# Feed-forward weights quantised in the first attention, sums added a step later, and smaller buffer rings

## What is computed

```python
x = x + L0_xattn(layernorm(x), ctx_1024, mask, ...)   # 16 heads of 64, 6272 keys, masked
x = x + L0_attn(layernorm(x), ...)
x = x + L0_ffn(layernorm(x), ...)                     # 8 experts, 2 chosen
x = x + L1_xattn(layernorm(x), ctx_1024, ...)         # 6272 keys, then 64 keys
x = x + L1_attn(layernorm(x), ...)                    # gated delta rule
x = x + L1_ffn(layernorm(x), W_in, b_in, W_out, b_out)

def quantize_w8_per(w, axis):                         # used by L1_ffn alone
    amax = jnp.clip(jnp.max(jnp.abs(w), axis=axis, keepdims=True), 1e-08, None)
    scale = 127.0 / amax
    return jnp.clip(jnp.round(w * scale), -128.0, 127.0) / scale
```

## Time and profile before

| | us |
|---|---|
| median of 3 executions | 407.27 |
| lowest and highest | 406.82 and 411.14 |
| profiled execution, its own time | 406.98 |
| span of the profile | 405.1 |
| PE matmul busy | 383.4 |
| ACT busy | 287.2 |
| DVE busy | 276.8 |
| POOL busy | 256.4 |

### The profile page before, as it was taken

One profiled execution on the slowest core, in us unless ns is written; L12 is line 12 of the kernel. 1 busy time (PEld: TensorE's weight loads), 2 busy tenths in 40 slices (PEclk: granted clock), 3 DMA queues, 4 the chain that ended last, 5 costly groups with the idle time before them and its releaser, 6 DMA issues.

```text
span 405.1 us, 11383 instructions
## 1 busy us (share of the span) xinstructions
PE 383.4 (95%) x4529; PEld 280.0 (69%) x4529; DVE 276.8 (68%) x715; ACT 287.2 (71%) x568; POOL 256.4 (63%) x207
## 2 busy tenths in 40 slices
PE   6988899999999999989999999998999999999996
PEld 3435677777777778954955767776777768867843
DVE  2796788888887776566767766676776666454544
ACT  3478768888888887646439988999888987534240
POOL 2489988999975659201007989999999879030000
PEclk9899999999999999999999999999999999999999
DMA  8899979999999999990006999999999999700000
GB/s 308 323 256 154 198 142 199 160 184 208 182 190 212 228 201 155 354 391 2 3 2 105 203 190 191 196 186 194 173 194 211 183 195 179 302 2 2 3 1 5
DMA packets 188389, 68.55 MB, mean 169 GB/s; under 512 B 183200, under 2 KB 183984, under 8 KB 187440
## 3 DMA queue, kind: packets, MB, share of 16 engines
q1 hardware_dynamic: 188048, 66.77, 82.1%
q10 hardware_dynamic: 288, 1.05, 0.7%
HBM read 21.90 MB, written 0.03 MB: 54 GB/s over the span
## 4 chain that ended last, share of the span: by engine, by line
PE 47%; POOL 19%; DMA 11%; DVE 9%; ACT 6%; issue 5%; SPq 0%; POOLq 0%; DVEq 0%; ACTq 0%
PE ps L522 16%; POOL halves L594 14%; PE ps L490 13%; DMA probsT<-halves 10%; DVE probs L641 3%; PE ps L1106 2%; PE ps L502 2%; PE ps L768 2%; ACT probs L559 2%; DMA moe<-in_ctxT 2%; ACT halves L566 2%; PE ps L1214 1%; PE ps L828 1%; PE ps L942 1%; PE ps L773 1%
## 5 line engine op out<-in xcount | busy, mean ns | idle before, releaser
L594 POOL TENSOR_TENSOR halves<-probs,halves 128x896 f16<-128x896 f32 x84 | 160.8, 1924 | 36.1 <-ACT halves L566 34.9
L522 PE MATMUL ps<-ctxN,probsT 128*128 128x128 f16 x2352 | 148.6, 219 | 5.9 <-DMA probsT<-halves 5.8
L522 PEld LDWEIGHTS ps<-ctxN,probsT 128*128 128x128 f16 x2352 | 139.0, 98 | 20.7 <-issue 10.4
L490 PE MATMUL ps<-ctxT_parts,GT_parts 128*128 128x512 f16 (+1 forms) x660 | 142.9, 353 | 3.7 <-DVE negmax L641 3.5
L559 ACT ACTIVATE probs<-probs,shifted 128x896 f32<-128x896 f32 x112 | 115.5, 1031 | 7.2 <-DVE shifted L646 7.2
L490 PEld LDWEIGHTS ps<-ctxT_parts,GT_parts 128*128 128x128 f16 x660 | 59.9, 98 | 54.4 <-DVE negmax L641 5.4
L566 ACT CAST halves<-probs 128x896 f16<-128x896 f32 x93 | 85.9, 923 | 0.1
L654 DVE SCALAR_TENSOR_TENSOR U<-U,alpha,ps 128x128 f32<-128x128 f32 x112 | 38.7, 345 | 60.4 <-PE ps L522 60.3
L641 DVE CUSTOM_DVE_ANT_0 probs<-ps,maskb,negmax 128x896 f32<-128x896 f32 x56 | 67.5, 1206 | 3.7 <-POOL halves L594 3.3
L641 DVE CUSTOM_DVE_ANT_0 probs<-ps,zero,negmax 128x896 f32<-128x896 f32 x56 | 67.5, 1206 | 2.1 <-POOL halves L594 1.6
L556 ACT ACTIVATE alpha<-negmax 128x1 f32<-128x1 f32 x96 | 28.3, 295 | 36.8 <-DVE negmax L641 36.3
(11 more groups left out here) (369 smaller groups left out, 381.2 us busy)
## 6 DMA issues: line engine op xcount, KB each, us to landing
moe<-in_ctxT SPq DMA_DIRECT2D x7, 448.0 KB, 7.5
moe<-in_mask SPq DMA_DIRECT2D x6, 448.0 KB, 9.9
moe<-in_gateT SPq DMA_DIRECT2D x2, 1024.0 KB, 9.2
moe<-in_upT SPq DMA_DIRECT2D x2, 1024.0 KB, 11.0
moe<-in_downT SPq DMA_DIRECT2D x2, 1024.0 KB, 12.6
moe<-in_fir_long SPq DMA_DIRECT2D x1, 2048.0 KB, 10.5
probsT<-halves SPq DMA_TRANSPOSE x93, 4.8
wv<-in_wv SPq DMA_DIRECT2D x2, 512.0 KB, 6.8
```

The source lines that it names most:

```text
L490: ins = pe.matmul(ps[:, 2 * b + h, 0:width], GT_parts[:, g_part, r * P:(r + 1) * P], ctxT_parts[:, keys:keys + width], start=(g_part == 0 ...
L522: ins = pe.matmul(ps[:, bank, 0:D], probsT_parts[:, b, p_part, k * P:(k + 1) * P], ctxN_parts[:, at:at + D], start=(p_part == 0 and c_part ...
L594: eng.tensor_tensor(halves_of(L, n)[:, 1, :], probs[:, n % BUFS, :], halves_of(L, n)[:, 0, :], ALU.subtract).then_inc(lower_of(L, n)[0], 1)
```

## The change

- The weights `win` and `wout` are loaded behind tiles 14 and 22 of attention 1 in place of 36 and 40, and two matrices of 512 KB for the next stage (`wqT1`, `wkT1`) change places with them.
- DVE takes the two maxima in its steps 32 and 33 of attention 1 and the scales in step 34.
- POOL quantises in attention 1, one instruction at every second tile from 35 to 49, and no longer in attention 2. The quantised weights get SBUF of their own, since the space that they had holds other data in attention 1.
- That space comes from the rings: 4 in place of 6 buffers of `probsT`, 5 in place of 7 of `halves`.
- `ADD_LAG` is 7 in place of 6: DVE adds the product of tile i-7 in its step i.

```diff
-BUFS, TURNED_BUFS, HALF_BUFS = 4, 6, 7
-PV_LAG, ADD_LAG = 5, 6
+BUFS, TURNED_BUFS, HALF_BUFS = 4, 4, 5
+PV_LAG, ADD_LAG = 5, 7
...
-        wqi = late(P, FT, D)
-        wqo = late(P, FT, D)
+        wqi = sb("wqi", [P, FT, D])[:]
+        wqo = sb("wqo", [P, FT, D])[:]
...
-        WEIGHTS_AT = {14: ("in1", w_qT, "wqT1"), 22: ("in1", wkT[:], "wkT1"), 30: ("out0", wv[:], "wv0"),
-                      34: ("small_attn", a_w[:], "a_w"), 36: ("ffn", win[:], "win"), 38: ("out0", wo[:], "wo0"),
-                      40: ("ffn", wout[:], "wout"), 44: ("delta", d_w[:], "d_w"), 46: ("delta", w1s[:], "w1s")}
+        WEIGHTS_AT = {14: ("ffn", win[:], "win"), 22: ("ffn", wout[:], "wout"), 30: ("out0", wv[:], "wv0"),
+                      34: ("small_attn", a_w[:], "a_w"), 36: ("in1", w_qT, "wqT1"), 38: ("out0", wo[:], "wo0"),
+                      40: ("in1", wkT[:], "wkT1"), 44: ("delta", d_w[:], "d_w"), 46: ("delta", w1s[:], "w1s")}
...
             for n in range(STEPS):
                 if not on_pe(0, n) and not on_vector(0, n):
                     lower(pool, 0, n)
                 denominators(pool, 0, n)
                 if n > (CH - 1) * RT:
                     last_denominator(pool, 0, n - 1)
                 if n == 1:
                     mask(1)
+                if 35 <= n < 51 and n % 2 == 1:
+                    quantise_weights((n - 35) // 8, (n - 35) // 2 % 4)
...
-                        if 12 <= n < 44 and n % 4 == 0:
-                            quantise_weights((n - 12) // 16, (n - 12) // 4 % 4)
...
-            flash_dve(dve, 0, {1: partial(g_lower_dve, dve, 0, slice(4 * P, 8 * P), 5)})
+            def weight_maxima(i):
+                loaded(dve, "ffn")
+                dve.tensor_reduce(wamx[:, i * FT:(i + 1) * FT], (win, wout)[i][:], AX, ALU.max,
+                                  apply_absolute_value=True).then_inc(sem("f_maxima"), 1)
+
+            def weight_scales():
+                dve.wait_ge(sem("f_maxima"), 2)
...
+            flash_dve(dve, 0, {1: partial(g_lower_dve, dve, 0, slice(4 * P, 8 * P), 5),
+                               32: partial(weight_maxima, 0), 33: partial(weight_maxima, 1), 34: weight_scales})
             turn_u_dve(dve, 0)
             project_dve(dve, 0)
-            loaded(dve, "ffn")
-            for i, w in enumerate((win, wout)):
-                ins = dve.tensor_reduce(wamx[:, i * FT:(i + 1) * FT], w[:], AX, ALU.max, apply_absolute_value=True)
-            seq(ins)
...
-            seq(dve.tensor_scalar(wamx[:], wamx[:], 1e-8, None, ALU.max))
-            seq(dve.reciprocal(wsc[:, 0, :], wamx[:]))
-            seq(dve.tensor_scalar(wsc[:, 0, :], wsc[:, 0, :], 127.0, None, ALU.mult))
-            dve.reciprocal(wsc[:, 1, :], wsc[:, 0, :]).then_inc(sem("f_scales"), 1)
```

More of the change, by code:

```diff
@@ L1409, in _ @@
             pool.wait_ge(sem("ctxT_ready"), 1)
[L1410 to L1429, removed]
             def quantise_weights(k, stage):
@@ L1443, in quantise_weights @@
                     pool.tensor_tensor(q, q, back, ALU.mult).then_inc(sem("f_wq"), 1)
+            ctxT_upper(1)
+            ctxT_lower(1)
+            for n in range(STEPS):
+                if not on_pe(0, n) and not on_vector(0, n):
+                    lower(pool, 0, n)
+                denominators(pool, 0, n)
+                if n > (CH - 1) * RT:
+                    last_denominator(pool, 0, n - 1)
+                if n == 1:
+                    mask(1)
+                if 35 <= n < 51 and n % 2 == 1:
+                    quantise_weights((n - 35) // 8, (n - 35) // 2 % 4)
+                c, part = 2 + (n - POOL_FROM) // 6, (n - POOL_FROM) % 6
+                if n >= POOL_FROM and c < CH:
+                    if part == 0:
+                        ctxT_upper(c)
+                    if part == 2:
+                        ctxT_lower(c)
+                    if part == 4:
+                        mask(c)
+            last_denominator(pool, 0, STEPS - 1)
             def keep_o1():
@@ L1615, in _ @@
             dve.wait_ge(sem("cleared"), 3)
-            flash_dve(dve, 0, {1: partial(g_lower_dve, dve, 0, slice(4 * P, 8 * P), 5)})
+            def weight_maxima(i):
[4 more added lines that the diff above has]
+                dve.wait_ge(sem("f_maxima"), 2)
+                seq(dve.tensor_scalar(wamx[:], wamx[:], 1e-8, None, ALU.max))
+                seq(dve.reciprocal(wsc[:, 0, :], wamx[:]))
+                seq(dve.tensor_scalar(wsc[:, 0, :], wsc[:, 0, :], 127.0, None, ALU.mult))
+                dve.reciprocal(wsc[:, 1, :], wsc[:, 0, :]).then_inc(sem("f_scales"), 1)
+            flash_dve(dve, 0, {1: partial(g_lower_dve, dve, 0, slice(4 * P, 8 * P), 5),
+                               32: partial(weight_maxima, 0), 33: partial(weight_maxima, 1), 34: weight_scales})
             turn_u_dve(dve, 0)
             project_dve(dve, 0)
-            loaded(dve, "ffn")
-            for i, w in enumerate((win, wout)):
-                ins = dve.tensor_reduce(wamx[:, i * FT:(i + 1) * FT], w[:], AX, ALU.max, apply_absolute_value=True)
-            seq(ins)
             loaded(dve, "par")
```

## The result

The changed kernel takes **411.57 us** (median of 20 runs, 410.86 to 412.62), the kernel before, run beside it, 406.98 (20 runs). The ratio is 1.0114, its 95% interval 1.0101 to 1.0128: slower by 1.1%, 4.6 us, where 4.3 less were forecast. The profiled executions are 411.69 us with a span of 409.9 and 406.98 with one of 405.1.

What follows compares the result with a forecast made beforehand. PE was taken as the bound, with POOL and ACT close behind and about 5.5 us of stalls in attention 2. The terms -4.1 - 0.8 + 0.35 + 0.3 = -4.25 gave 402.7 us from 406.98, range 400.3 to 406.2.

Steps and rivals of the forecast that it cites:

- I cost it at nothing: DVE's later additions: product waiting for an addition costs nothing; up to 0.6 us per tile whose turned lower half stands between.
- -4.1 us: Attention 2: of 4.5 us of PE stalls besides the one at tile 6, 4.1 us go.
- 1.4 us of earlier issue exceed every single stall: Attention 2: turnings leave 1.4 us earlier, more than any single stall, 1.0 us at most.
- the gate: Four turned buffers: turning n waits for product n-4. Rival: this closes a loop, kernel slower, 413.4 us, chance 0.05.
- The lead: DVE's next maximum no longer waits behind a product just ended, so tiles start earlier, by at most 1.33 us.
- SP is seldom the last in line today: Turnings before the change: a free one leaves when POOL is done, at tile 39 to the hundredth (308.64).
- -0.8: Attention 1: PE's waits for turnings and maxima, 1.1 us at most, shrink through later additions by 0.8 us.
- 2.7 us at most: Attention 1, steps 32 to 34: DVE's two maxima and four scales take this much over three steps, taken as hidden.
- +0.35: End of attention 1: POOL's last multiplication stands ahead of lower half 50; costs 0.35 us, between 0 and 1.05.
- +0.3: Attention 1: larger loads behind tiles 36 and 40 push turnings behind them; costs 0.3 us, between 0 and 2.8.
- The unbuilt lead: Rival: ACT is the bound that takes DVE's place, only POOL's lateness goes; 406.3 us, chance 0.18.
- Attention 1 in full: Rival: both loads late on tiles without spare time (2.8 us), POOL's end unrelieved (1.05); 405.9 us, chance 0.11.

Runs made afterwards that it cites:

- experiment 3: Five turned and six half buffers in place of four and five, against the changed kernel: 410.80 us, ratio 1.0101.
- experiment 4: Turning of the lower halves by DMA left out, product reads the upper half twice, against the changed kernel: 403.90 us, ratio 0.9934.
- experiment 6: Additions back at six steps in place of seven, against the changed kernel: 410.79 us, ratio 1.0108.

## Why the prediction was wrong, step by step

**"I cost it at nothing" (additions a step later): this step failed.** It named the place, "a tile whose turned lower half stands between", and gave it up to 0.6 us each, DVE's own time. The runs show 3.5 us at the two ends. Not DVE's work costs but its wait: at the end the transposes of tiles 53 and 55 come behind the product that has just been made, so the half waits for PE and ACT, and the addition for the half. One must ask of what stands ahead in the queue not how long it takes, but what it waits for. With this undone alone the kernel still takes 407.92 us. Forecast and result lie 8.9 us apart: 3.5 here, 4.0 in the next step, 0.9 in the loads and 0.4 in POOL's last multiplication make nearly all of it.

**"-4.1 us" (attention 2): its step "1.4 us of earlier issue exceed every single stall" failed.** It came out at -0.1: -0.6 up to product 48 and +0.5 from there to product 50. The issue was not earlier. Tile 39 in the changed kernel, on POOL, PE and SP:

```profile
307.12 1.89 POOL L594 TENSOR_TENSOR halves<-probs,halves 128x896 f16<-128x896 f32 x1 [0.41 <-ACT halves L566]
...
308.29 1.34 PE L522 MATMUL ps<-ctxN,probsT 128*128 128x128 f16 x21
...
309.22 1.90 SPq L421 DMA_TRANSPOSE probsT<-halves  x1
...
311.21 2.32 SPq L421 DMA_TRANSPOSE probsT<-halves  x1
```

The lower half is ready at 309.01, product 35, the gate, ends at 309.63. But SP is still issuing turning 38 (309.22 + 1.90), and turning 39 leaves at 311.21, 1.58 us after the gate and 6.68 before its product (317.89). In the earlier trace rows it left 6.74 us before its product. So it is with each of the 43 turnings of tiles 6 to 48: by the records of POOL, PE and SP, SP is the last in line in all of them, and they leave 1.9 us in the mean after both the lower half and the gate. Before, 32 of the 43 left more than 0.15 us after them. (The view of SP's waits puts some 50 us in either kernel down to POOL's lower halves; those are mostly the lower halves of later tiles, finished while SP issues.) The lead came, and became a queue ahead of SP. The prediction read tile 39 of before, which left 0.03 us after POOL was done with SP free since 308.42, and took it for the rule. "SP is seldom the last in line today" was argued from that one tile.

The bound could have been read from the kernel before, from SP's 92.9 us of issuing in 100. In the changed kernel, where SP goes from one issue to the next in 0.1 us (once in 0.45), the turnings of tiles 6 to 48 leave 2.40 us apart, against PE's 2.31 us a tile. A turning moves 128 x 1792 x 2 bytes, 448 KB, so that is 191 GB/s. (The 190 GB/s of the earlier trace rows don't show it by themselves: 43 tiles in 104.94 us ask for 188 GB/s whatever limits them.) The Trainium skill (DMA: Bandwidth & Descriptors, section Latency and other measured facts) gives transposing transfers 261 GB/s, measured on one kernel with a non-contiguous middle dimension, with which a turning would take some 1.76 us (estimate) and a quarter of the time would be spare. The runs speak against it here: 191 GB/s with SP issuing all the time.

**"-0.8" (attention 1):** the size was near, 1.47 alone and 0.92 in the change, within the caution above; 0.55 are lost again at product 29, which waits for an addition behind DVE's four scales. For these "none dearer than that", 0.68 us, was too low: one takes 1.50, and the four together last from 105.52 to 107.7 us. Nor does "2.7 us at most" follow from it: two maxima and four scales of up to 0.68 us make 4.1.

**"+0.35" (POOL's last multiplication)** came out at +0.78, at products 49 and 50. The path was another: not lower half 50, its turning and product 50, but lower half 50, DVE's maximum 54 and the additions queued behind it (experiment 3). And it was not by POOL alone: with five and six buffers, POOL's work unchanged, it is gone. **"+0.3" (the loads)** is +1.23, within the bound of 2.8; 0.7 of it hang on the smaller rings.

**The rivals.** The unbuilt lead is refuted (1.3 us of waits, and 2.31 us a tile in experiment 4). The gate closes no loop: five buffers leave attention 2 as it is. Its sign was right, its mechanism wrong. Attention 1 in full had 2.8 us for the loads and 1.05 for POOL's end, where 1.23 and 0.78 were measured.

**The signs.** Two of being wrong came: PE waits eight times for turnings in attention 2, and products 37 and 41 of attention 1 are late. Of being right, DVE's wait fell to 1.3 us, but turning 39 left 1.58 us behind its gate, not 0.2. ACT's waits before copies, up to 0.9 us, stayed under the 1.4 named.

As to the instruction transfers, they number 36 again, on the same row of the page as the earlier trace rows, and long landings again reach 6.8 us. That the one lengthens the other was not tried.

What stays open is whether SP's issue or the transfers behind it fill up first. The shortest issue, 1.30 us, and the 1.22 of experiment 4 speak for the transfers.

## What to carry to other kernels

Before you cost an earlier start, add up how long the issuing queue is busy in that stretch: work made ready sooner gains nothing where the transfers follow each other without a gap, and giving a few tiles to another way does. Where an instruction is moved back behind others, look at the first and last tiles of the loop, where these others wait for something else than in the middle. And move parts of a change one at a time: here a lead that was good in one attention came with a queue that cost more at both ends.

## What the hardware did that I had not expected

An operation of 8 columns on DVE took some ten times as long beside POOL. In the kernel before, with POOL idle:

```profile
185.90 0.17 DVE L1683 TENSOR_SCALAR wamx<-wamx 128x8 f32<-128x8 f32 x1
```

The changed kernel's timeline of POOL and DVE:

```profile
105.51 1.92 POOL L594 TENSOR_TENSOR halves<-probs,halves 128x896 f16<-128x896 f32 x1
105.52 0.16 DVE L1623 TENSOR_SCALAR wamx<-wamx 128x8 f32<-128x8 f32 x1
...
105.96 1.50 DVE L1625 TENSOR_SCALAR wsc<-wsc 128x8 f32<-128x8 f32 x1
...
107.50 0.20 DVE L1626 RECIPROCAL wsc<-wsc 128x8 f32<-128x8 f32 x1
```

The second of the same shape ends at 107.46, 0.03 us after POOL's subtraction. In experiment 6 it was the first one, 1.86 us to 109.71, with POOL's subtraction ending at 109.69. The Trainium skill (SBUF — State Buffer, section SBUF: two separate sides) says that VectorE in some modes and GpSimd share a pair of ports by an exclusive lock, held for the whole instruction, while the other blocks. These two rows agree with it; that 0.16 us at 105.52 slipped through beside the same subtraction, and 0.74 at 109.98 beside another operation of POOL, no run here explains.
